# Attention-value products of two graph-attention stages: column groups of 64 queries in place of 32

## The chip, the cores and the metric

One Trainium2 chip, one core. The metric is the device time of one execution in microseconds, the median of several runs.

## What is computed

64 graphs of 128 nodes with 256 features pass through two layers. Both use dense attention over the 128 nodes of a graph, with 8 heads of 32 features in the first two of three attentions. The part that matters here, cut from the reference:

```python
# layer 0 (transformer block), N = 128, H = 8, Hd = 32
weights = softmax(logits, axis=-1) * (0.25 + 0.75 * adj)
weights = weights / jnp.maximum(weights.sum(axis=-1, keepdims=True), 1e-06)
attended = jnp.einsum('bhnm,bhmd->bhnd', weights, v)        # attention-value product 1
...
# layer 1 (graph attention, called twice: 8 heads of 32, then 1 head of 256)
e = leaky_relu(s[:, :, :, None] + t[:, :, None, :], 0.2) + bias[:, None, :, :]
attn = softmax(e, axis=-1)
out = jnp.einsum('bhij,bhjk->bhik', attn, h)                # attention-value product 2 (8 heads)
```

## The kernel before

The whole input stays in SBUF. NC = 16 chunks of G = 4 graphs pass through four stages, one after the other; each engine has its own instruction stream, written out by hand, and the streams meet at semaphores.

- **Stage A** is layer 0's attention (about 40 to 409 us of the profile). In each chunk, two passes (`pp`) of two graphs go through logits (L1428), maxima and exponentials on DVE and ACT, transposes of the weights (`a_turn`, L1435), a multiplication by the adjacency factors into `pt_sb` on DVE (L507), the attention-value product `a_av` (L1447), normalisation, a transpose (`a_attn_turn`, L1454) and the output projection `a_out` (L1461). The projections to query, key and value of the next chunk (`wide`, `tall`, L1332 to L1350) lie between them on TensorE. `a_av` is called once for each of the 64 graphs.
- **Stage B** is the feed-forward part (409 to about 760 us), **stage C1** the 8-head graph attention (about 780 to 971 us), **stage C2** the 1-head graph attention and the output (to the end).
- **Stage C1** is a software pipeline over the 16 chunks. In one step `c1_step` TensorE does, in this order: `ratios` (L1595) for heads 0 to 3 of the chunk before; the score rows `c_st` (L1332 to L1334); `c_av` (L1611) for heads 4 to 7 of the chunk two before, called the far products here; `ratios` for heads 4 to 7, which writes the same PSUM banks and so waits until DVE has read the first four heads (`c_pp`, written at L695); two of four projections; the transposes of the layer norm (L1357) and of the rows (L1585); `c_av` for heads 0 to 3 of the chunk before, called the near products here; the other two projections (L1348 to L1350). `c_av` is called once for each head of each chunk, and does all 4 graphs of the chunk.

Both products have one form: the weights of one head of one graph, 128 keys x 128 queries in fp32, are the stationary operand; the values of that head and graph with a column of ones behind them (HA = 33 columns) stream through it. The 128 queries are cut into 4 column groups of 32: each group is a matmul with a `tile_position` of its own in the columns of the array, and writes its own 32 partitions of PSUM. Each such fp32 matmul of the program appears in the trace as two pairs of a weight load (PEld, LDWEIGHTS) and a matmul (PE, MATMUL). One graph of stage A therefore has 8 heads x 4 groups x 2 = 64 pairs, and four heads of one chunk in C1 have 4 x 4 graphs x 4 groups x 2 = 128 pairs.

Of the kernel before, what the change touches and what calls it, by code (L numbers as in the profile page):

```python
# [34 lines left out]
HD = D // H  # L35
# [12 lines left out]
def wait_for(eng, sem, value):  # L48

    if isinstance(value, int) and value <= 0:  # L50
        return
    eng.wait_ge(sem, value)


def build(nc, x, adj, wq, bq, wk, bk, wv, bv, wo, bo, g1, b1, g2, b2, wf1, bf1, wf2, bf2,
# [7 lines left out]
    with ctx:  # L63
# [1265 lines left out]
        def _(pe):  # L1329
# [108 lines left out]
            def a_av(s, sp, i, par, pp, g):  # L1438

                pe.wait_ge(a_vev, i * 2 + 2)  # L1440
                pe.wait_ge(a_pt, sp * 4 + 4)
                wait_for(pe, a_ac, s)
                for h in range(H):
                    j, at = 4 * (h % 4) + 2 * g + h // 4, ((2 * pp + g) * H + h) * HA
                    for c in range(4):
                        rows = slice(c * HD, (c + 1) * HD)
                        m = pe.matmul(O_ps[rows, h, :], pt_sb[pp][:, j, rows], v_sb[par][:, at:at + HA],  # L1447
                                      start=True, stop=True, tile_position=(0, c * HD))
                m.then_inc(a_o, 1)

            def a_attn_turn(s):
# [12 lines left out]
            def a_step(i, half, par):  # L1464
                first, tail = (isinstance(i, int) and i == n for n in (0, NC))
                for pp in range(2):
# [15 lines left out]
                    if back:  # L1482
                        a_av(s - 2, sp - 1, *before, 0)
# [18 lines left out]
                    if back:  # L1502
                        a_av(s - 1, sp - 1, *before, 1)
                        a_out(s - 2)
# [16 lines left out]
            for i in range(NC):  # L1521
                a_step(i, i // 2, i % 2)
            a_step(NC, NC // 2, 0)
            a_av(NG - 2, NG // 2 - 1, NC - 1, 1, 1, 0)
            a_out(NG - 3)
            a_attn_turn(NG - 2)
# [71 lines left out]
            def c_av(i, par, h):  # L1598
                k = h // 3
                first, heads = HEAD_GROUPS[k]  # L1600
                pe.wait_ge(c_pp, i * H + h + 1)
                if h == 0:
                    pe.wait_ge(c_hb, i * 2 + 2)
                    pe.wait_ge(c_one, i + 1)
                if h == first:
                    wait_for(pe, c_ev, i * len(HEAD_GROUPS) + (k - 1))
                for g in range(G):
                    at = (g * heads + h - first) * HA
                    for c in range(4):
                        rows = slice(c * HD, (c + 1) * HD)  # L1610
                        r = pe.matmul(BK[rows, 4 + (par + k) % 2, at:at + HA], pp[h][:, g, rows],  # L1611
                                      hb[par][:, (g * H + h) * HA:(g * H + h + 1) * HA],
                                      start=True, stop=True, tile_position=(0, c * HD))
                r.then_inc(c_o, 1)

            def c_h_out(g, par):
# [4 lines left out]
            def c1_step(i, half, par):  # L1621
                back = not (isinstance(i, int) and i == 0)
                far = back and not (isinstance(i, int) and i == 1)
                if back:
                    pe.wait_ge(ln_xl, (i + CC) * KT + 2)
                    ratios(i - 1, 1 - par, 0)
                    pe.wait_ge(c_hb, i * 2)
                    c_st(i, 0, par)
                    c_st(i, 1, par)
                if far:  # L1630
                    for h in range(4, H):
                        c_av(i - 2, par, h)
                if back:
                    ratios(i - 1, 1 - par, 1)
                c_h_out(0, par)
                c_h_out(1, par)
                if back:
                    c1_turn(i + 1)
                else:
                    pe.wait_ge(b_x, NG)  # L1640
                row_turn(i, par)
                if back:
                    for h in range(4):
                        c_av(i - 1, 1 - par, h)
                pe.wait_ge(c_one, i + 1)
                c_h_out(2, par)
                c_h_out(3, par)
# [10 lines left out]
            for h in range(4, H):  # L1658
                c_av(NC - 2, 1 - last, h)
# [100 lines left out]
```

## Time and profile before

| | us |
|---|---|
| median of 3 runs | 1109.23 (1108.74 to 1109.35) |
| span of the profiled execution | 1100.2 |
| TensorE busy (PE) | 1042.0 (95%) |
| weight loads (PEld) | 912.7 (83%) |
| VectorE busy (DVE) | 803.3 (73%) |
| ScalarE busy (ACT) | 714.7 (65%) |
| L1447, 4096 pairs, share of PE's busy time | 48.8 |
| L1611, 4096 pairs, share of PE's busy time | 46.7 |

The span runs from the first to the last instruction; what lies around it is 9.0 us. PE is TensorE's matmuls, PEld its weight loads, which overlap the matmuls. The duration of one matmul in the profile runs from its start until its last result is out; matmuls that follow each other overlap, so a duration is not the time that one costs: that is the distance between two starts. In a merged line such as "0.77 PE L1447 ... x64" the 64 starts lie within 0.77 us less the duration of the last one.

### The profile page before, as it was taken

The page shows a single profiled execution, that of the slowest core. Times are in us where ns is not written, and L with a number is a line of the kernel's source. Part 1 is how long each engine was busy: PE and PEld are TensorE (multiplying, and loading weights), DVE is VectorE, ACT ScalarE, POOL GpSimd, SP SyncE. Part 2 cuts the span into 40 slices and gives each one's busy share as a digit, 9 for nine tenths or more (in the row PEclk, how much of TensorE's full clock was granted, in tenths as well). Part 3 has the DMA queues.
Part 4 walks back from the last instruction along what each step waited for, and adds up shares of the span by engine and source line. Part 5 has one row for each costly group of instructions (what it writes and reads, how often), then busy time and mean ns, then how long its engine had stood idle before and what let it go on. Part 6 is the DMA issues. An engine that isn't in the chain of part 4 may idle for free.

```text
span 1100.2 us, 39179 instructions
## 1 busy us (share of the span) xinstructions
PE 1042.0 (95%) x15924; PEld 912.7 (83%) x15924; DVE 803.3 (73%) x1935; ACT 714.7 (65%) x1718; POOL 398.2 (36%) x628
## 2 busy tenths in 40 slices
PE   6999999999999989999999999999899999879997
PEld 5888888888888868899989998998778888768886
DVE  4677777777777768865566556655788899859986
ACT  2777667777767755564455445546688888847774
POOL 3531121121121103331123112212478788776552
PEclk9999999999999999999999999999999999989999
DMA  9211111221110002110011011010000000002212
GB/s 246 51 42 41 41 41 41 65 55 41 41 41 12 12 2 59 30 29 20 24 30 25 20 25 30 24 39 10 22 22 19 19 29 20 4 2 78 78 62 93
DMA packets 82476, 43.67 MB, mean 40 GB/s; under 512 B 42912, under 2 KB 77984, under 8 KB 82336
## 3 DMA queue, kind: packets, MB, share of 16 engines
q1 hardware_dynamic: 78016, 41.44, 13.9%
q8 instruction: 98, 1.61, 0.6%
q10 hardware_dynamic: 4320, 0.28, 0.3%
q14 instruction: 42, 0.34, 0.1%
HBM read 21.25 MB, written 12.58 MB: 31 GB/s over the span
## 4 chain that ended last, share of the span: by engine, by line
PE 79%; DVE 8%; issue 5%; POOL 3%; ACT 2%; SPq 1%; DMA 1%; DVEq 0%; POOLq 0%; ACTq 0%
PE BK L1332 8%; PE BK L1334 8%; PE BK L1333 8%; PE BK L1461 6%; PE BK L1435 5%; PE BK L1548 5%; PE BK L1549 5%; PE BK L1550 5%; PE BK L1447 4%; PE BK L1428 3%; PE BK L1348 3%; PE BK L1357 3%; PE BK L1595 3%; PE BK L1349 2%; PE BK L1350 2%
## 5 line engine op out<-in xcount | busy, mean ns | idle before, releaser
L1180 ACT ACTIVATE gf<-BK,bcol 128x512 f32<-128x512 f32 x128 | 88.3, 690 | 159.0 <-PE BK L1334 145.9
L953 POOL TENSOR_TENSOR ve<-mv,eps_l 128x4 f32<-128x4 f32 x64 | 18.3, 285 | 450.4 <-DVE mv L314 418.1
L1096 ACT ACTIVATE e_sb<-BK,nmx 128x128 f32<-128x128 f32 x512 | 142.5, 409 | 28.3 <-DVE nmx L501 28.3
L597 DVE TENSOR_TENSOR gl<-gf,gh 128x512 fp32r<-128x512 f32 x128 | 101.2, 793 | 67.6 <-ACT gh L1181 65.4
L1548 PE MATMUL BK<-wf_hi,gh 128*128 128x256 f32 x512 | 142.5, 278 | 1.8 <-DVE gl L597 1.8
L1549 PE MATMUL BK<-wf_hi,gl 128*128 128x256 f32 x512 | 141.5, 276 | 0.0
L1550 PE MATMUL BK<-wf_lo,gh 128*128 128x256 f32 x512 | 141.5, 276 | 0.0
L507 DVE TENSOR_TENSOR pt_sb<-BK,ft 128x512 f32<-128x512 f32 x128 | 85.2, 686 | 59.8 <-PE BK L1435 58.1
L1116 ACT ACTIVATE xn<-x_all,neg_mr,rstd 128x256 f32<-128x256 f32 (+1 forms) x188 | 103.9, 611 | 4.8 <-POOL neg_mr L962 4.4
L1332 PE MATMUL BK<-xh,wf_hi 128*128 128x512 f32 x256 | 99.8, 390 | 1.3 <-DVE xl L341 0.8
L1334 PE MATMUL BK<-xh,wf_lo 128*128 128x512 f32 x256 | 100.8, 394 | 0.0
L1333 PE MATMUL BK<-xl,wf_hi 128*128 128x512 f32 x256 | 100.5, 392 | 0.0
L501 DVE TENSOR_REDUCE nmx<-BK 128x8 f32<-128x1024 f32 x64 | 76.7, 1219 | 30.4 <-PE BK L1428 30.4
L1548 PEld LDWEIGHTS BK<-wf_hi,gh 128*128 128x128 f32 x512 | 96.1, 188 | 3.3 <-DVE gl L597 2.6
L1549 PEld LDWEIGHTS BK<-wf_hi,gl 128*128 128x128 f32 x512 | 96.2, 188 | 0.7
L1550 PEld LDWEIGHTS BK<-wf_lo,gh 128*128 128x128 f32 x512 | 96.2, 188 | 0.0
L309 DVE BATCH_NORM_STATS2 st<-x_all 128x6 f32<-128x256 f32 (+1 forms) x256 | 90.7, 410 | 5.2 <-DMA x_all<-in_x_dram 4.7
L695 DVE SCALAR_TENSOR_TENSOR pp<-BK,gt_all 128x512 f32<-128x512 f32 x128 | 81.9, 682 | 16.8 <-PE BK L1595 16.8
L934 POOL TENSOR_TENSOR x_all<-x_all,bo_bc 128x256 f32<-128x256 f32 x64 | 44.7, 732 | 131.1 <-ACT xn L1116 118.9
L934 POOL TENSOR_TENSOR x_all<-x_all,c_bc 128x256 f32<-128x256 f32 (+1 forms) x128 | 90.1, 740 | 4.3 <-ACT xn L1116 2.6
L1181 ACT ACTIVATE gh<-BK,bcol 128x512 fp32r<-128x512 f32 x128 | 87.3, 682 | 0.0
L1435 PE MATMUL BK<-ident,e_sb 128*128 128x128 f32 x512 | 73.2, 276 | 1.6 <-ACT e_sb L1096 1.3
(206 smaller groups left out, 2762.9 us busy)
## 6 DMA issues: line engine op xcount, KB each, us to landing
x_all<-in_x_dram SPq DMA_DIRECT2D x16, 512.0 KB, 4.7
out_dram<-y SPq DMA_DIRECT2D x16, 512.0 KB, 2.9
xn<-tb_ln SPq DMA_DIRECT2D x240, 32.0 KB, 1.9
adj_in<-in_adj_dram SPq DMA_DIRECT2D x64, 64.0 KB, 3.5
adj_kept<-adj_tr SPq DMA_DIRECT2D x16, 256.0 KB, 2.4
adj_in<-adj_kept SPq DMA_DIRECT2D x16, 256.0 KB, 2.6
s_wf<-in_L_gnn_Wf_dram SPq DMA_DIRECT2D x2, 1024.0 KB, 6.8
s_w<-in_L_gnn_W_dram SPq DMA_DIRECT2D x2, 256.0 KB, 2.9
```

The lines of the kernel that those rows point to most:

```text
L309: dve.bn_stats(st[:, g, :], xs(i, g)).then_inc(ln_st, 1)
L597: dve.tensor_tensor(gl[:, f, :], gf[f % 2][:], gh[:, f, :].bitcast(F32), ALU.subtract).then_inc(b_gl, 1)
L934: pool.tensor_tensor(xs(i, g), xs(i, g), bias[:], ALU.add).then_inc(signal, 1)
L1096: e = act.activation(e_sb[:, j, :], LE[:, r, q, :], ACT.Exp, bias=nmx[:, j:j + 1], scale=1.0)
L1116: act.activation(xn[:, g, :], xs(nxt, g), ACT.Identity, scale=rstd[:, g:g + 1], bias=neg_mr[:, g:g + 1]).then_inc(ln_xn, 1)
L1332: pe.matmul(dst, w_hi, m_hi, start=start, stop=False)
L1333: pe.matmul(dst, w_hi, m_lo, start=False, stop=False)
L1334: return pe.matmul(dst, w_lo, m_hi, start=False, stop=stop)
L1435: m = pe.transpose(LE[:, r, q, :], e_sb[:, 4 * r + q, :], ident[:])
L1548: pe.matmul(dst, gh[:, f, n], hi[:, f, :], start=(f == 0), stop=False)
L1549: pe.matmul(dst, gl[:, f, n], hi[:, f, :], start=False, stop=False)
L1550: r = pe.matmul(dst, gh[:, f, n], lo[:, f, :], start=False, stop=(f == FT - 1))
```

## The change

Each product is cut into 2 column groups of 64 queries instead of 4 groups of 32, in `a_av` and in `c_av`. The same elements of PSUM are written with the same sums. The number of matmuls is halved (8 for each pair of graph and head become 4 pairs in the trace's count), each has a stationary operand of 64 columns, and the moving operand stays at 33 columns. No wait, no semaphore and no order changes.

```diff
--- before.py
+++ after.py
@@ -1442,10 +1442,10 @@
                 wait_for(pe, a_ac, s)
                 for h in range(H):
                     j, at = 4 * (h % 4) + 2 * g + h // 4, ((2 * pp + g) * H + h) * HA
-                    for c in range(4):
-                        rows = slice(c * HD, (c + 1) * HD)
+                    for c in range(2):
+                        rows = slice(c * 2 * HD, (c + 1) * 2 * HD)
                         m = pe.matmul(O_ps[rows, h, :], pt_sb[pp][:, j, rows], v_sb[par][:, at:at + HA],
-                                      start=True, stop=True, tile_position=(0, c * HD))
+                                      start=True, stop=True, tile_position=(0, c * 2 * HD))
                 m.then_inc(a_o, 1)
 
             def a_attn_turn(s):
@@ -1606,11 +1606,11 @@
                     wait_for(pe, c_ev, i * len(HEAD_GROUPS) + (k - 1))
                 for g in range(G):
                     at = (g * heads + h - first) * HA
-                    for c in range(4):
-                        rows = slice(c * HD, (c + 1) * HD)
+                    for c in range(2):
+                        rows = slice(c * 2 * HD, (c + 1) * 2 * HD)
                         r = pe.matmul(BK[rows, 4 + (par + k) % 2, at:at + HA], pp[h][:, g, rows],
                                       hb[par][:, (g * H + h) * HA:(g * H + h + 1) * HA],
-                                      start=True, stop=True, tile_position=(0, c * HD))
+                                      start=True, stop=True, tile_position=(0, c * 2 * HD))
                 r.then_inc(c_o, 1)
 
             def c_h_out(g, par):
```

## Rows read from the trace of the kernel before

**Rows 1.** The page's first lines: span, and busy time of each engine.
```profile
span 1100.2 us, 39179 instructions
PE 1042.0 (95%) x15924; PEld 912.7 (83%) x15924; DVE 803.3 (73%) x1935; ACT 714.7 (65%) x1718; POOL 398.2 (36%) x628
```

**Rows 2.** Busy time in stretches: stage, length, engines' busy us (count), granted clock.
```profile
core 0: us, PE busy (x) PEld busy (x) DVE busy (x) ACT busy (x) POOL busy (x), PEclk, DMA share, GB/s
43.00:409.00 366.00, 357.34 (x6778) 303.94 (x6771) 278.20 (x610) 262.81 (x782) 75.40 (x123) 1.00 0.15 39
786.00:975.00 189.00, 175.18 (x5702) 153.34 (x5701) 162.82 (x367) 155.15 (x334) 144.15 (x239) 0.98 0.07 18
```

**Rows 3.** The same view: one chunk's step of stage A, and one of C1.
```profile
149.99:173.65 23.66, 23.39 (x433) 19.98 (x433) 18.16 (x40) 17.20 (x51) 4.42 (x9) 1.00 0.23 54
835.76:847.63 11.87, 11.26 (x363) 9.79 (x362) 10.65 (x25) 10.24 (x23) 9.70 (x17) 1.00 0.09 22
```

**Rows 4.** PE's groups by line: shapes, count, busy us, mean ns of one, idle before.
```profile
L1447 PE MATMUL BK<-v,pt_sb 128*32 128x33 f32 x4096 | 48.8, 198 | 3.3 <-DVE pt_sb L507 0.8 <-ACT att_t L1102 0.6
L1611 PE MATMUL BK<-hb,pp 128*32 128x33 f32 x4096 | 46.7, 201 | 1.2 <-issue 1.2
L1447 PEld LDWEIGHTS BK<-v,pt_sb 128*32 128x32 f32 x4096 | 42.1, 109 | 14.0 <-issue 12.1
```

**Rows 5.** Timeline around one product of stage A: start us, us, engine, line, count.
```profile
197.34 1.09 PE L1357 MATMUL BK<-ident,xn 128*128 128x128 f32 x8
198.37 0.65 PEld L1447 LDWEIGHTS BK<-v,pt_sb 128*32 128x32 f32 x64 [0.17 <-issue]
198.37 0.77 PE L1447 MATMUL BK<-v,pt_sb 128*32 128x33 f32 x64
199.06 0.73 PEld L1461 LDWEIGHTS BK<-wo_sb,att_t 128*128 128x128 f32 x4
199.06 1.13 PE L1461 MATMUL BK<-wo_sb,att_t 128*128 128x256 f32 x4
```

**Rows 6.** The same product's weight loads: first 32, then the last 31.
```profile
198.37 0.35 PEld L1447 LDWEIGHTS BK<-v,pt_sb 128*32 128x32 f32 x32 [0.17 <-issue]
...
198.65 0.37 PEld L1447 LDWEIGHTS BK<-v,pt_sb 128*32 128x32 f32 x31
```

**Rows 7.** Timeline, end of stage B: fp32 matmuls with 128-column weights.
```profile
741.88 0.97 PEld L1363 LDWEIGHTS BK<-cols,wc 128*128 128x128 f32 x8
741.99 0.95 PE L1363 MATMUL BK<-cols,wc 128*128 128x1 f32 x8
...
742.79 1.97 PE L1378 MATMUL BK<-s_w,lb_wide 128*128 128x256 f32 x8
```

**Rows 8.** Mean ns of one weight load and one matmul, for the same two lines.
```profile
L1363 PEld LDWEIGHTS BK<-cols,wc 128*128 128x128 f32 x8 | 1.0, 191 | 0.0
L1378 PE MATMUL BK<-s_w,lb_wide 128*128 128x256 f32 x8 | 2.0, 390 | 0.0
L1595 PEld LDWEIGHTS BK<-row_c,inv 4*128 4x128 f32 x1024 | 31.9, 186 | 16.7 <-DVE pp L695 8.3 <-issue 6.3
```

**Rows 9.** Timeline of a C1 step: near products, ratios, far products, the wait.
```profile
835.76 1.36 PE L1611 MATMUL BK<-hb,pp 128*32 128x33 f32 x128
...
837.05 0.38 PE L1348 MATMUL BK<-w_hi,xh 128*128 128x256 f32 x1
...
838.67 0.98 PEld L1595 LDWEIGHTS BK<-row_c,inv 4*128 4x128 f32 x32
838.67 1.17 PE L1595 MATMUL BK<-row_c,inv 4*128 4x128 f32 x32
...
841.37 1.46 PE L1611 MATMUL BK<-hb,pp 128*32 128x33 f32 x128
842.08 1.28 DVE L695 SCALAR_TENSOR_TENSOR pp<-BK,gt_all 128x512 f32<-128x512 f32 x2
...
843.41 1.17 PE L1595 MATMUL BK<-row_c,inv 4*128 4x128 f32 x32 [0.59 <-DVE pp L695]
```

**Rows 10.** Waits between 800 and 960 us: total us, times, longest us.
```profile
PE BK L1595 <- DVE pp L695: 7.8, 13, 0.8
```

**Rows 11.** PE's timeline at the end of C1: the last far products.
```profile
968.40 2.00 PE L1611 MATMUL BK<-hb,pp 128*32 128x33 f32 x128
970.95 0.35 PE L1677 MATMUL BK<-w_hi,xh 128*128 128x258 f32 x1 [0.55 <-ACT o_sb L1284]
```

## The prediction

> **What bounds the kernel now.** I read the engines' busy shares first: TensorE is busy for 95% of the span, and no other engine comes near it [rows 1]. A share over the whole span hides stages, so the next view is the busy time of the two stages that the change touches. In stage A, TensorE has 357.3 of 366 us, DVE 278 and ACT 263 [rows 2]; one chunk's step of 23.66 us leaves TensorE 0.27 us idle [rows 3]. What TensorE gains or loses there goes into the time one for one. In stage C1 the margin is smaller: in a step of 11.87 us TensorE is busy for 11.26, DVE for 10.65, ACT for 10.24 [rows 3], so TensorE's place in the step has to be looked at. The granted clock is 1.00 in stage A and in the steps shown, which is the 2.4 GHz level, and the change makes TensorE neither idle nor sparse, so I leave it at that level.
>
> Then the products themselves. The groups by line give each of the two 4096 pairs [rows 4]. Their mean duration (198 ns) is no price, because they overlap; the price is in the timeline. One graph of stage A has its 64 matmuls in 0.77 us, and the next line's work starts at 199.06, before the last result is out [rows 5]. First start to last start is 0.77 - 0.20 = **0.57 us**. Four heads of one chunk in C1 (128 pairs) take 1.36 - 0.20 = **1.16 us** as near products and 1.46 - 0.20 = **1.26 us** as far products [rows 9].
>
> **What sets the pace of a product.** The four column groups work side by side: one graph and head needs, in each group, two pairs of load and matmul, one after the other. I call the time in which every group does one pair a round. A graph of stage A has 8 heads x 2 = 16 rounds, four heads of a chunk have 4 x 4 x 2 = 32. This number does not change: after the change a round has 2 pairs of 64 columns instead of 4 pairs of 32, but there are still 16 and 32 of them. So the halved count of matmuls pays nothing by itself, unless a round gets shorter.
>
> A round now: the first 32 weight loads start within 0.35 - 0.11 = 0.24 us, which is 7.7 ns each, 31 ns for a round of four; the last 31 start within 0.26 us, 8.7 ns each, 35 ns for a round [rows 6]. The mean over the whole product is 0.57 / 16 = 36 ns, the uncovered first load included. Two things could set the 31 ns. Streaming 33 rows: the 8 matmuls with 256 rows start within 1.97 - 0.39 = 1.58 us, 226 ns each, 0.88 ns for a row [rows 7, 8], so 33 rows take 29 ns. Loading 32 columns: the 8 matmuls of one row follow loads of 128 columns, which start within 0.97 - 0.19 = 0.78 us, 111 ns each, 0.87 ns for a column [rows 7, 8], so 32 columns take 28 ns. One is hidden behind the other, and a round is a little over the longer. Today both are alike.
>
> **The change, step by step.** (1) The stream stays at 33 rows, 29 ns. (2) The load goes to 64 columns. No row shows a load of 64, so it is bounded from both sides: from below by half of a 128-column load, 111 / 2 = 55.5 ns, if it runs alone at 0.87 ns a column; from above by twice the present mean round, 71 ns. That loads in different tiles do run side by side at their own column count is seen in `ratios`, where 32 loads of 128 columns in four row tiles start within 0.98 - 0.19 = 0.79 us: 25.6 ns each, 102 ns for four [rows 8, 9], and not 4 x 111. On the straight line from 31 ns at 32 columns to 102 to 111 ns at 128 columns, 64 columns lie at 55 to 58 ns. I take **57.5 ns**: the load, no longer the stream, sets the round. (3) The issue of instructions, which seems to pace the second half of a product at 8.7 ns a pair, falls out: a pair may now take 57.5 / 2 = 29 ns.
>
> Stage A: 16 rounds x 57.5 = 0.92 us for a graph, against 0.57: +0.35 us. Sixty-four graphs: **+22.4 us**, all exposed since TensorE has 0.27 us of idle time in a step of four graphs [rows 3]. The change of mode ahead of each product (0.17 us without a load in [rows 5]) and behind it stays as it is, at no cost or gain.
>
> Stage C1, near products: 32 x 57.5 = 1.84 us against 1.16: +0.68. Behind them the projections follow at once, at 837.05 [rows 9], and then `ratios`, for which DVE waits: nothing covers it. Sixteen chunks: **+10.9 us**. The bound from below is that DVE's and ACT's streams take the step over, but DVE has 1.2 us free in a step [rows 3], more than 0.68.
>
> Stage C1, far products: 1.84 against 1.26: +0.58 us. Here TensorE stands still afterwards: `ratios` for heads 4 to 7 waits 0.59 us for DVE's fourth scaling [rows 9], in 13 of the steps 7.8 us in all [rows 10]. DVE's chain up to that point (`ratios`, scalings, row minima) does not pass through the far products, so the wait shrinks to about nothing and hides the loss: **0**. If that cover were gone, it would cost 0.58 x 16 = 9.3 us. The last far products of the stage have no such wait behind them; a copy by ACT and stage C2 follow [rows 11]: **+0.6 us**.
>
> Sum: 22.4 + 10.9 + 0.6 = 33.9 us. The profiled span of 1100.2 becomes 1134.1. The median of the runs lies 9.0 us above the span, and the change does not touch what lies around it: 1109.2 + 33.9 = **1143 us**, 3.1% slower.
>
> With 55.5 ns a round the sum is 0.318 x 64 + 0.61 x 16 = 30.2 us (1139); with 62 ns, twice the present round of 31, it is 0.42 x 64 + 0.82 x 16 + about 2 of the far products = 42 (1151).
>
> **Rivals.** (a) *The rate is simply halved.* If what sets the round is not the load but some share of the array that each group owns, two groups do half the work of four, and each product takes twice as long: +0.57 x 64 + 1.16 x 16 + (1.26 - 0.59) x 14 = 64 us, **1174**. For it speaks that the present round (36 ns in the mean) is longer than both of its parts; against it that the surplus over 28 ns comes in good part from issue and from the first load, which do not double. The Trainium skill states this rule in "TensorEngine Tiling (Array Packing)", Performance Considerations: a stationary side of up to 32 packs four tiles, one of up to 64 only two. It speaks against the change as the rows do.
>
> (b) *A 64-column load takes no longer than a 32-column load*, because the array fills in strips of 32 side by side. Then the round is set by the stream and stays at 31 ns, without the slower second half: 16 x 31 = 0.50 against 0.57 and 0.99 against 1.16, -0.07 x 64 - 0.17 x 16 = -7.2 us, **1102**. Its place is the weight load; it decides from the point where a round is under 36 ns. For it: the present 31 ns could as well be the stream's 29 as the load's 28. Against it: the 128-column loads show 111 ns, not 28 [rows 7], and they fill the same strips.
>
> (c) *Each pair has a fixed price.* If 0.57 us is 64 times 8.9 ns, half the pairs cost half: -0.285 x 64 - 0.58 x 16 = -27.5 us, **1082**. The even 8.7 ns of the second half speaks for it; against it, one group cannot take its 33 rows in less than 29 ns, so 16 rounds need 0.46 us. The Trainium skill has such a price in the same page, Instruction Overhead: some 60 cycles for each matmul, however small. By it, at 2.4 GHz, 64 matmuls would take 1.6 us (an estimate from that page), where the trace has 0.57; the trace disagrees for tiles side by side.
>
> (d) *Load and stream no longer overlap, or the two groups do not run side by side.* The first gives a round of 57.5 + 29 = 86 ns: 0.81 x 64 + 1.59 x 16 + 0.90 x 14 = 90 us, **1199**. The second gives 115 ns: 1.27 x 64 + 2.52 x 16 + 1.83 x 14 = 147, **1256**. Nothing in the trace speaks for either: row tiles of 128 columns overlap both [rows 9].
>
> **How the numbers follow.** The forecast with its spread, 1134 to 1160: 0.82. (a) 0.05, (b) 0.04, (c) 0.01, (d) 0.05 together, and 0.03 for a gain of rounds and cover that cancels out within 0.2%, which is about what a measurement of this kernel can tell from no change. The range leaves out (a) to (d) and the case of no change, 0.18 in all, and reaches from 1134 (a round of 55.5 ns, and half of the near products' 9.8 us covered by waits that I do not see) to 1160 (a round of 62 ns, and the far products not covered at all: 0.42 x 64 + 0.82 x 16 + 0.72 x 16 = 51.5 us). Slower by over 0.2%: 0.92; faster: 0.05; the same: 0.03.
>
> **What would show it.** L1447 and L1611 with 2048 pairs each and forms of 64 columns (with 32 columns the change would not be there). Weight loads of one product 29 ns apart, the mean duration of one up by about 28 ns from 109. One product of stage A at 0.92 us between first and last start, the step of stage A at 25.1 us. In C1, near products at 1.84 us, the wait of L1595 for DVE near 0, the step at 12.55 us. I am wrong if loads stand at 16 ns (b), or if the wait in C1 stays and the step is longer all the same.

## The result, and the profile after

| | before | after |
|---|---|---|
| median of the runs, us | 1108.99 (1104.75 to 1109.35) | 1132.38 (1128.57 to 1135.67) |
| ratio, with its 95% interval | | 1.0231 (1.0197 to 1.0265) |
| span of the profiled execution, us | 1100.2 | 1127.8 |

The kernel became slower: by the ratio 25.6 us (22 to 29), between the two profiled executions 27.6 us. The prediction was 33.9 us and 1143 us, with a range from 1134; the direction and the mechanism hold, the amount was too large by a quarter (profiles) to a third (ratio). The median lies 1.6 us below the range; the ratio, put on the 1109.2 us from which the prediction started, gives 1135 us, just inside it. One thing has to be known to read the totals: stage B, which the change does not touch, takes 362.4 us in some executions and 368.4 in others (the last line of the next views shows the long one, in `e1_a_only` below), so totals scatter by some 6 us, and what follows compares each stage with itself.

The page of the changed kernel, first lines, to be held beside [rows 1]:

```profile
span 1127.8 us, 30987 instructions
PE 1085.0 (96%) x11828; PEld 961.8 (85%) x11828; DVE 804.4 (71%) x1935; ACT 718.1 (64%) x1718; POOL 398.0 (35%) x628
```

8192 instructions are gone, and TensorE is busy for 43 us longer. The busy time in stretches, here cut at the borders of stages B, C1 and C2, first before, then after, then stage B of `e1_a_only` (columns as in [rows 2]):

```profile
773.60:970.90 197.30, 181.32 (x5791) 158.47 (x5789) 170.87 (x384) 161.55 (x345) 147.11 (x244) 0.98 0.07 19
411.20:773.60 362.40, 358.32 (x2341) 324.52 (x2340) 228.60 (x519) 187.91 (x307) 91.35 (x111) 1.00 0.11 28
970.90:1100.20 129.30, 111.52 (x816) 96.85 (x816) 102.93 (x361) 83.01 (x244) 72.54 (x128) 0.97 0.19 66
```

```profile
429.60:792.10 362.50, 358.67 (x2342) 324.81 (x2341) 228.65 (x519) 187.88 (x307) 91.37 (x111) 1.00 0.11 28
792.10:1000.10 208.00, 204.06 (x3743) 182.41 (x3742) 172.36 (x384) 162.66 (x345) 147.00 (x244) 0.97 0.06 17
1000.10:1127.80 127.70, 111.84 (x816) 97.34 (x816) 102.35 (x361) 82.89 (x244) 72.57 (x128) 0.95 0.19 67
```

```profile
429.30:797.70 368.40, 364.30 (x2342) 330.25 (x2341) 228.63 (x519) 187.61 (x307) 91.30 (x111) 1.00 0.11 27
```

So stage A, which ends at 429.6 instead of 411.2, lost 18.4 us; stage B nothing; C1 208.0 - 197.3 = 10.7 us. C2 is 1.6 us shorter without having been changed.

Now the products. Two lines of the groups by line, as in [rows 4], and the timeline around one product of stage A, as in [rows 5]:

```profile
L1447 PEld LDWEIGHTS BK<-v,pt_sb 128*64 128x64 f32 x2048 | 65.4, 138 | 14.0 <-issue 12.1
...
L1447 PE MATMUL BK<-v,pt_sb 128*64 128x33 f32 x2048 | 72.0, 224 | 3.3 <-DVE pt_sb L507 0.8 <-ACT att_t L1102 0.6
```

```profile
205.75 1.01 PEld L1447 LDWEIGHTS BK<-v,pt_sb 128*64 128x64 f32 x32 [0.17 <-issue]
205.75 1.13 PE L1447 MATMUL BK<-v,pt_sb 128*64 128x33 f32 x32
...
206.80 1.13 PE L1461 MATMUL BK<-wo_sb,att_t 128*128 128x256 f32 x4
```

Half the pairs, but the matmuls start 1.13 - 0.22 = 0.91 us apart from first to last, 0.91 / 31 = 29 ns each, so a round of two takes 58 ns, as forecast (57.5). The next line starts 206.80 - 205.75 = 1.05 us after the product, where it was 199.06 - 198.37 = 0.69 [rows 5]: a product costs **0.36 us** more. Loads have gone from 109 to 138 ns each, the 29 ns that 32 more columns take.

TensorE's timeline in C1, as in [rows 9]: near products, ratios, far products, ratios.

```profile
857.02 2.06 PE L1611 MATMUL BK<-hb,pp 128*64 128x33 f32 x64
859.00 0.38 PE L1348 MATMUL BK<-w_hi,xh 128*128 128x256 f32 x1
...
860.62 1.17 PE L1595 MATMUL BK<-row_c,inv 4*128 4x128 f32 x32
...
863.32 2.06 PE L1611 MATMUL BK<-hb,pp 128*64 128x33 f32 x64
865.36 1.17 PE L1595 MATMUL BK<-row_c,inv 4*128 4x128 f32 x32
```

From the near products to the next line it is now 859.00 - 857.02 = 1.98 us against 1.29 [rows 9]: +0.69. From the far products to the ratios it is 865.36 - 863.32 = 2.04 us, and it was 843.41 - 841.37 = 2.04: +0. The line of the wait [rows 10] is down to one time:

```profile
PE BK L1595 <- DVE pp L695: 0.7, 1, 0.7
```

One more view, which the prediction did not use: the waits of the weight loads (PEld) in stage A, before and after (line, what it waited for, total us, times, longest us; 60 to 380 us of the span before, 60 to 400 after).

```profile
PEld BK L1447 <- issue: 9.1, 40, 0.3
PEld BK L1428 <- issue: 8.7, 27, 0.4
PEld BK L1435 <- ACT e_sb L1096: 5.4, 13, 0.4
PEld BK L1357 <- ACT v L1087: 2.5, 13, 0.2
```

```profile
PEld BK L1447 <- issue: 9.2, 41, 0.3
PEld BK L1428 <- issue: 8.7, 27, 0.4
PEld BK L1357 <- ACT v L1087: 2.5, 13, 0.2
```

Once in each step, 13 times in the window, the loads of the first transposes (L1435) stood 0.4 us waiting for ACT's exponentials. After the change that line is gone. It is the same cover as in C1, in a stage in which I had found none. The timeline behind the product of [rows 5] shows how much of the price it takes, first before, then after:

```profile
200.21 0.42 PEld L1435 LDWEIGHTS BK<-ident,e_sb 128*128 128x128 f32 x4 [0.42 <-ACT e_sb L1096]
...
200.62 0.48 PE L1332 MATMUL BK<-xh,wq_hi 128*128 128x512 f32 x1
```

```profile
207.59 0.55 PEld L1435 LDWEIGHTS BK<-ident,e_sb 128*128 128x128 f32 x4
...
208.13 0.47 PE L1332 MATMUL BK<-xh,wq_hi 128*128 128x512 f32 x1
```

From the start of the product to these loads it is 1.84 us in both kernels (200.21 - 198.37 and 207.59 - 205.75): the longer product only fills the wait. To the projection behind the transposes (L1332) it is 2.38 us instead of 2.25, so 0.13 us of this product's 0.36 is left.

### The profile page after: what moved, and what is told of

Same layout as the page of the kernel before. It is cut to its first block, busy times and chain, and to the rows that moved or that the text cites. A ratio compares the mean times of both kernels' runs of the same rounds, so it can differ in the third digit from the quotient of the medians.

```text
span 1127.8 us, 30987 instructions
## 1 busy us (share of the span) xinstructions
PE 1085.0 (96%) x11828; PEld 961.8 (85%) x11828; DVE 804.4 (71%) x1935; ACT 718.1 (64%) x1718; POOL 398.0 (35%) x628
## 4 chain that ended last, share of the span: by engine, by line
PE 81%; DVE 7%; issue 4%; POOL 3%; ACT 2%; SPq 1%; DMA 1%; POOLq 0%; DVEq 0%; ACTq 0%
PE BK L1332 8%; PE BK L1334 8%; PE BK L1333 8%; PE BK L1461 6%; PE BK L1447 6%; PE BK L1548 5%; PE BK L1549 5%; PE BK L1550 5%; PE BK L1435 5%; PE BK L1611 4%; PE BK L1428 3%; PE BK L1357 3%; PE BK L1348 3%; PE BK L1595 3%; PE BK L1350 2%
## 5 line engine op out<-in xcount | busy, mean ns | idle before, releaser
L1332 PE MATMUL BK<-xh,wf_hi 128*128 128x512 f32 x256 | 99.9, 390 | 1.0 <-DVE x_all L523 0.5
L1447 PEld LDWEIGHTS BK<-v,pt_sb 128*64 128x64 f32 x2048 | 65.4, 138 | 14.0 <-issue 12.1
```

Source lines behind the costliest of these rows:

```text
L1332: pe.matmul(dst, w_hi, m_hi, start=start, stop=False)
```

## The experiments

**The theory.** (1) A round lasts as long as the longer of load and stream; a load costs what its columns cost, and two groups of 64 make the load the longer one. (2) The price of a product counts only where no wait of TensorE stands behind it: the far products of C1 and one of four products in stage A are covered. The rivals: the price is paid everywhere or shared evenly; load and stream follow each other; each pair has a fixed price. Edits are against the kernel before unless another is named. A step of stage A is read as the distance between two lines of L1357, one of which stands in each step; before it is 23.66 us, from 197.34 [rows 5] to

```profile
221.00 1.09 PE L1357 MATMUL BK<-ident,xn 128*128 128x128 f32 x8
```

**One stage alone.** `e1_a_only` has the first hunk of the change, `e2_c_only` the second.

> Two groups of 64 in stage A alone; C1 keeps four groups of 32. Theory: each of the 64 products costs 0.36 us more (0.90 us between first and last start against 0.57, and 0.03 us more behind it), and 0.24 us of the 1.45 us in a step of four comes back, because TensorE's wait for ACT's exponentials ahead of the first transposes of the step goes away: step of 24.87 us instead of 23.66, stage A 18.5 us longer, 1127 us. Rival, no cover anywhere in stage A: step of 25.1 us, 23 us longer, 1132 us.

> Two groups of 64 in stage C1 alone; stage A keeps four of 32. Theory: the near products cost 0.67 to 0.69 us a step, the far products nothing, since the wait of the ratios for DVE (0.59 us) takes them up: step of 12.53 us instead of 11.87, C1 about 11 us longer, 1120 us. Rival, far products cost as well: step of 13.1 us, 1129 us.

Measured: e1 1.0153 (1.0101 to 1.0205), e2 1.0072 (1.0048 to 1.0095) of the kernel before on the same chip (1105 us there): +16.9 and +8.0 us. Their sum, 24.9, is the whole change's 25.6 within the intervals. Stage A of e1, in the timeline:

```profile
204.32 1.09 PE L1357 MATMUL BK<-ident,xn 128*128 128x128 f32 x8
...
229.19 1.09 PE L1357 MATMUL BK<-ident,xn 128*128 128x128 f32 x8
```

24.87 us a step: the theory's number, and not 25.1. In e2 a step of C1, from near products to near products, is 12.55 us:

```profile
844.53 2.06 PE L1611 MATMUL BK<-hb,pp 128*64 128x33 f32 x64
...
850.82 2.06 PE L1611 MATMUL BK<-hb,pp 128*64 128x33 f32 x64
852.86 1.17 PE L1595 MATMUL BK<-row_c,inv 4*128 4x128 f32 x32
...
857.08 2.06 PE L1611 MATMUL BK<-hb,pp 128*64 128x33 f32 x64
```

The rival's 13.1 us is out: far products cost nothing. Both totals lie under the expected sums in microseconds, in part because these were reckoned from 1109 us; as differences 16.9 and 8.0 stand against 18.5 and 11. The 18.5 lies within e1's interval; the 11 lies above e2's (5 to 10.5 us), although its step is right: from the first near products to the first line of C2 (L1677) e2's profile has 192.5 us against 184.2 before, +8.3. Where the rest of C1's price went is told with the prediction below.

**Covered against uncovered products.** The same change, sorted by what stands behind the product:

```diff
 def a_av(s, sp, i, par, pp, g):
...
+    w = 64 if (pp, g) == (1, 0) else 32      # e3_covered; e4_uncovered: 32 and 64 exchanged
...
-        for c in range(4):
-            rows = slice(c * HD, (c + 1) * HD)
+        for c in range(P // w):
+            rows = slice(c * w, (c + 1) * w)
...
 def c_av(i, par, h):
...
+    w = 64 if h >= 4 else 32                 # e3_covered; e4_uncovered: 32 and 64 exchanged
...
```

Lines are left out where the dots stand: `c_av` has the same loop, and `tile_position` goes by `w` in both.

> Groups of 64 only where a wait stands behind the product: the first of the four products in a step of stage A, and the far products (heads 4 to 7) of C1. Theory: stage A +0.36 - 0.24 = +0.12 us a step, C1 +0 in the loop and +0.6 at its end, +2.6 us in all, 1112 us. Rival, price without cover: 0.36 x 16 + 0.6 x 16 = 15 us, 1124 us.

> Groups of 64 only where nothing stands behind the product: the other three products of a step of stage A, and the near products (heads 0 to 3) of C1. Theory: 3 x 0.36 = +1.08 us a step of stage A with its wait for ACT still there, +0.67 us a step of C1 with its wait for DVE still there, 16.5 + 10.7 = 27 us, 1136 us, and so close to the changed kernel. Rival, the loss is spread over all products evenly: 3/4 of 18.5 and half of 10.7, 19 us, 1128 us.

Measured: e3 0.9987 (0.9959 to 1.0014), no difference that can be told from none (-4.5 to +1.5 us, below the +2.6 expected); e4 1.0225 (1.0171 to 1.0279), as slow as the whole change. Half of C1's products can have the dear form for nothing in the loop (in e3 a step is 852.34 - 840.48 = 11.86 us, before 11.87), and a quarter of stage A's for 0.13 us a step. The steps of stage A in e3 and in e4:

```profile
198.71 1.09 PE L1357 MATMUL BK<-ident,xn 128*128 128x128 f32 x8
...
222.50 1.09 PE L1357 MATMUL BK<-ident,xn 128*128 128x128 f32 x8
```

```profile
203.76 1.09 PE L1357 MATMUL BK<-ident,xn 128*128 128x128 f32 x8
...
228.49 1.09 PE L1357 MATMUL BK<-ident,xn 128*128 128x128 f32 x8
...
854.48 1.46 PE L1613 MATMUL BK<-hb,pp 128*32 128x33 f32 x128
856.53 1.17 PE L1596 MATMUL BK<-row_c,inv 4*128 4x128 f32 x32 [0.59 <-DVE pp L695]
```

23.79 us in e3 (+0.13 for one product) and 24.73 us in e4 (+1.07 for three, 0.36 each). Together +1.20, the whole change's step (24.87 - 23.66 = 1.21). In e4 the far products (L1613 there, with the ratios at L1596) keep their old length, and the wait of 0.59 us behind them is there again.

**The load alone, larger.** `e5_one_group` has one group of 128 queries in both products.

> One group of 128 queries in both stages: a load of 128 columns for each pair. Theory, the load sets the round at 0.87 ns a column: a round of 111 to 114 ns, a product of stage A 1.8 us, of C1 3.6 us; +1.2 x 64 - 4 in stage A, +2.45 x 16 near, +1.9 x 14 far: about 140 us more, 1250 us. Rival, each pair has a fixed price of 29 ns: 16 pairs in 0.46 us, faster than before, near 1100 us. Rival, the rate goes with the number of groups and not with the columns (31 at four groups, 58 at two): one group 116 ns, not to be told from the theory here.

One product of stage A in the timeline (L1448 there), its loads and its matmuls, and two stretches of C1 in the view of busy time:

```profile
220.72 1.86 PEld L1448 LDWEIGHTS BK<-v,pt_sb 128*128 128x128 f32 x16
...
220.83 1.87 PE L1448 MATMUL BK<-v,pt_sb 128*128 128x33 f32 x16
```

```profile
860.00:880.00 20.00, 20.00 (x212) 19.20 (x205) 13.70 (x30) 12.37 (x28) 12.21 (x21) 0.86 0.09 28
880.00:900.00 20.00, 20.00 (x126) 18.97 (x124) 8.24 (x20) 8.17 (x16) 7.05 (x12) 0.59 0.00 1
```

1268.82 us, in one run. The loads of a product of stage A start within 1.86 - 0.19 = 1.67 us (0.19 is the last one's own duration), 1.67 / 15 = 111 ns a pair with 33 rows behind each load, as reckoned (111 to 114): a fixed price of a pair (0.46 us a product) is out, and the load goes on growing with its columns. The third rival, 116 ns by the number of groups, is too near to be told apart here; against it speaks `ratios`, with loads of 128 columns in four row tiles and 102 ns a round [rows 8, 9], but no run has column groups whose number and width change separately. That the time still passed the 1250 expected lies in C1 (from its first near products to the first line of C2 291.2 us, before 184.2: +107 instead of 66), and there a lower clock had a part: the granted clock, 1.00 in [rows 3], falls to 0.86 and 0.59 in the stretches shown (a mixture of the two levels), though TensorE's records leave no gap. A step of C1 takes 16.76 us (865.02 to 881.78), but three of the first twelve take 24.59 (as from 881.78 to 906.37, at a granted clock of 0.58).

**The stream alone, larger.** Stage A only; heads 0 to 6 stream 66 columns. `e6_32x66` with four groups of 32, `e7_64x66` with two groups of 64.

```diff
-    m = pe.matmul(O_ps[rows, h, :], pt_sb[pp][:, j, rows], v_sb[par][:, at:at + HA],
+    n = HA if h == H - 1 else 2 * HA
+    m = pe.matmul(BK[rows, 4, h * HA:h * HA + n], pt_sb[pp][:, j, rows], v_sb[par][:, at:at + n],
...
```

This is cut to the matmul; `e7_64x66` has the loop over two groups of the change as well.

> Stage A alone: four groups of 32 as before, but 66 columns stream through for heads 0 to 6 (the next head's values as well, whose sums the next head overwrites: work added, none left out). Theory, a round is the longer of load (28 ns) and stream (58 ns): 58 to 61 ns for 14 of 16 rounds, a product of 0.87 to 0.91 us, 1126 us. Rival, load and stream one after the other: 86 ns, a product of 1.27 us, 1150 us. Rival, the round goes with the number of groups alone: 31 to 36 ns, 1109 us.

> Stage A alone: two groups of 64, and 66 columns stream through for heads 0 to 6 (the next head's values as well, whose sums the next head overwrites). Theory, load of 64 columns (56 to 58 ns) and stream of 66 rows (58 ns) lie over each other: a round of 58 to 62 ns, a product of 0.90 to 0.96 us, 1127 to 1130 us. Rival, the 58 ns of the changed kernel are half load and half stream, one after the other: 87 ns, a product of 1.28 us, 1150 us.

One product of stage A in the timeline of e6, then of e7:

```profile
216.92 1.07 PE L1447 MATMUL BK<-v,pt_sb 128*32 128x66 f32 x64
```

```profile
217.24 1.12 PE L1447 MATMUL BK<-v,pt_sb 128*64 128x66 f32 x32
```

1121.94 and 1126.74 us, one run each. With small loads, twice the stream costs nearly what twice the load does (1.07 - 0.19 = 0.88 us). With loads of 64 columns, twice the stream costs nothing: 1.12 us against 1.13 in the changed kernel with 33 columns, and e7's step is e1's, 24.87 us (204.32 to 229.20, within 0.01). Load and stream lie over each other and the longer one sets the round; were they in series, the product of e7 would take 1.28 us.

**The wait in stage A by itself.** `e8_order` leaves the groups at 32 and moves a projection ahead of the transposes that wait for ACT; `e9_order_64` does the same to the changed kernel.

```diff
                         if pp == 0:
                             if first:
                                 pe.wait_ge(setup_dve, setup_at["splits"])
+                            a_proj(i, 0)
                         else:
                             a_proj(i, 3)
                     if not first:
                         a_turn(sp, 0)
-                    if pp == 0 and not tail:
-                        a_proj(i, 0)
```

> Groups of 32 as before; the first query projection of a step of stage A goes ahead of the first four transposes of the weights, which wait for ACT's exponentials. Theory: the 0.24 us that the change got back from this wait are to be had without it: step of 23.4 us instead of 23.66, 3.5 us faster, 1105.5 us. Rival: DVE, which scales behind these transposes, takes the place of ACT, since its first scaling comes 1.4 us later: no gain, 1109 us.

> The changed kernel (two groups of 64 in both stages) with the order of e8_order in stage A. Theory: the longer first product already covers the wait ahead of the transposes, so there is nothing left for the order to gain: step of stage A 24.85 to 25.0 us, as in the changed kernel (24.87), although the same order gave 0.11 us a step with groups of 32. Rival, order and group size add up: 24.76 us a step.

The ratio of e8 is 0.9973 (0.9947 to 1.0000). Its step of stage A comes first, then the one wait of its weight loads (60 to 380 us) that is new; no line of L1435 is left among them:

```profile
267.96 1.09 PE L1357 MATMUL BK<-ident,xn 128*128 128x128 f32 x8
...
291.51 1.09 PE L1357 MATMUL BK<-ident,xn 128*128 128x128 f32 x8
```

```profile
PEld BK L1332 <- DVE xl L326: 2.9, 13, 0.2
```

23.55 us a step, a gain of 0.11 us and not of 0.24. Neither the theory's number nor the rival's: the wait for ACT is gone, but the projection (L1332) stands in its place with a wait of 0.2 us of its own, for DVE's split of the normalised input (`xl`). In all that is 16 x 0.11 = 1.8 us, which the ratio cannot tell for certain from nothing; it is the only version here whose step is shorter than that of the kernel before. In e9 (one run, 1130.81 us) the step is 24.86 us, as in the changed kernel:

```profile
255.62 1.09 PE L1357 MATMUL BK<-ident,xn 128*128 128x128 f32 x8
...
280.48 1.09 PE L1357 MATMUL BK<-ident,xn 128*128 128x128 f32 x8
```

With the longer product in front, the order has nothing left to gain. The same quarter of a microsecond cannot be won twice.

## Why the prediction was right or wrong, step by step

- **What sets the pace: right.** A round of 58 ns against the 57.5 taken from the straight line between 32 and 128 columns. e5, e6 and e7 show the three sides of it: load larger, stream larger, both larger. The rivals by a halved rate, by load and stream in series and by groups that do not run side by side fall with that number, the fixed price with e5, the load for nothing with the 138 ns of one load. That columns and not the number of groups decide is argued and not shown (e5).
- **Stage A, price of a product: right.** 0.36 us against 0.35. Of it 0.03 us lies behind the product and not in it: the next line starts 153 ns after the last matmul's start instead of 126. I had that at zero.
- **Stage A, "all exposed": wrong, and this is the step that failed.** I read the 0.27 us that TensorE is idle in a step [rows 3] as leaving no room for cover. TensorE's records hide the wait: those of the output projection run to 199.06 + 1.13 = 200.19 us, while its loads end at 199.06 + 0.73 = 199.79 [rows 5] and the next loads stand until 200.21 for ACT, 0.42 us. Of the 1.45 us that four products cost, 24.87 - 23.66 = 1.21 us stayed in the step and 0.24 came back: 16 x 0.24 = 3.8 us. From 64 x 0.36 = 23.0 this leaves 19.2; the stage lost 18.4. The other 0.8 us lies at its two ends: the 14 whole steps between them lost 16.8 us (from the line of L1357 at 55.32 us to that at 386.69 before, from 55.52 to 403.66 after), the first and the last step 1.6 together instead of 2.4; why, I did not trace.
- **C1, near products: right.** 0.69 us against 0.68, nothing behind them to cover it. **Far products: right.** 0 against 0, by the cover that was named, and e4 shows the cover come back when the products shrink. The stage lost 10.7 us against 10.9 + 0.6, and that the sums lie so close is in part luck. From the first to the fifteenth near products the loop lost 7.9 us (786.77 to 954.21 before, 806.85 to 982.16 after) and not 14 x 0.69 = 9.7: the profile of before has one long step there, 13.44 us (798.61 to 812.05), in which TensorE stands still for 1.34 us without a cause that the profile shows, and the changed kernel has none. The way into the loop, on the other hand, took 1.6 us longer, the end of the stage 1.2.
- **The last far products: mis-sized.** Forecast at +0.6 us; the next line comes 1000.11 - 995.94 = 4.17 us after their start, and 970.95 - 968.40 = 2.55 in [rows 11], +1.6. Between 995 and 1000 us the granted clock is 0.50 (before, between 965 and 971 us, 0.58).

```profile
995.94 3.63 PE L1611 MATMUL BK<-hb,pp 128*64 128x33 f32 x64
1000.11 0.55 PE L1677 MATMUL BK<-w_hi,xh 128*128 128x258 f32 x1 [0.54 <-issue]
```

- **The clock: right in stage A and in the loop of C1.** 1.00 in the steps of both. Over all of C1 it is 0.97, where it was 0.98: the end of the stage, as just told, runs at the lower level in part, before and after.
- **What lies around the span: wrong, without weight in the sum.** I read the 9.0 us between the span and the median as time around the span. The profiled run of the changed kernel took 1129.7 us with a span of 1127.8, so 1.9 us lies around it; in every run on record it is 1.8 to 2.2. The median belongs to executions with a longer span than the profiled one. That most of the other 7 us is stage B's longer length is likely, since the profiled execution of before has the short one, but no profile of such an execution of before shows it.
- **The total.** 33.9 forecast; 18.4 + 10.7 - 1.6 = 27.5 in the profiled pair. The cover in stage A explains 3.8 of the 6.4 us between them, C1's sum 0.8, and stage C2's 1.6 is scatter: the profiles give as much among kernels in which it is the same (127.6 to 129.3 us). The lower end of the range, 1134, was built from half of C1's price; the cover that was really there lay in stage A, and I had left no room for it.

## What to carry to other kernels

Counting matmuls is no price: with column groups side by side, find the round, and ask whether load or stream is the longer one in it; in fp32, where a loaded column and a streamed row cost about the same here (0.87 and 0.88 ns), a stationary operand that grows past the rows streamed through it makes the load the bound. To see whether a busy TensorE hides a wait, look at the waits of its weight loads and not at its idle time, since tails of matmuls count as busy (0.27 us idle and 0.42 us of waiting in the same step here). And price a product by the distance from its start to the start of the next line, then ask for each place what that next line waits for.

## What the runs showed of the hardware that I had not expected

In e5, TensorE's records leave no gap in most of C1 (290.00 of 290 us from 845 to 1135), and still the granted clock fell to 0.86 and 0.59 in the stretches shown. In the second of them 11.0 us go to pairs of a 128-column load and 33 rows:

```profile
L1613 PE MATMUL BK<-hb,pp 128*128 128x33 f32 x64 | 11.0, 345 | 0.0
```

In stage A of the same kernel, where 16 such pairs stand between other work instead of 32, the clock was 1.00 from 200 to 400 us. What in this decides was not tried; it does show that a TensorE busy by its records can be at the lower clock. And stage B ran at two paces, 362.4 us and 368.4 us, at a granted clock of 1.00 in both; what chooses between them these runs do not show.
